# A graph and mixture-of-experts layer on one core: a helper matrix built on ScalarE, edge scatters started earlier, end-of-pass parts cut finer, a third buffer in the last stage, and seven slot one-hots in one comparison

## The reference, cut to what matters

```python
x0 = layernorm(x)
# graph: two hypergraph convolutions, four segment sums in all
m  = segment_sum((h @ W)[src], dst) / count(dst)     # then
h' = prelu(segment_sum(m[dst], src) / count(src) + b)
# linear attention over the nodes: k, v normalised per head, out = q (k^T v) / n
# mixture of experts on layernorm(x + graph + attention):
#   8 experts, the best 2 per token, y = sum_j w_j * (gelu(xn @ W1[e_j] + b1) @ W2[e_j] + b2)
```

## Time and profile before

| | |
|---|---|
| median of 3 runs | 5673.13 us (5672.77 to 5675.39) |
| profiled execution | 5671.47 us |
| its span | 5669.7 us |
| POOL busy | 3808.1 us (67%) |
| PE busy | 4272.6 us (75%) |
| DVE busy | 2923.7 us (52%) |
| ACT busy | 1244.4 us (22%) |
| mean granted PE clock | 0.878 |

### The profile page before, as it was taken

One profiled execution on the slowest core, in us unless ns is written; L12 is line 12 of the kernel. 1 busy time (PEld: TensorE's weight loads), 2 busy tenths in 40 slices (PEclk: granted clock), 3 DMA queues, 4 the chain that ended last, 5 costly groups with the idle time before them and its releaser, 6 DMA issues. The chain is left out here.

```text
span 5669.7 us, 68658 instructions
## 1 busy us (share of the span) xinstructions
PE 4272.6 (75%) x18010; PEld 2970.2 (52%) x18011; DVE 2923.7 (52%) x10203; ACT 1244.4 (22%) x3306; POOL 3808.1 (67%) x3968
## 2 busy tenths in 40 slices
PE   4799899999997878776566666655666665658994
PEld 2545566666665555554444444444444444445662
DVE  8788777777874555544333333333333333373334
ACT  0388655555531000000100000000000000132331
POOL 2777777777767777777677777777777777303442
PEclk9899999999998999897788888887778778778997
DMA  3400233333343333334454454344333333421115
GB/s 127 134 5 2 61 105 105 105 105 105 104 153 111 114 113 112 114 109 126 129 146 143 145 147 147 115 132 142 105 105 105 105 105 105 147 81 49 63 63 164
DMA packets 322940, 616.68 MB, mean 109 GB/s; under 512 B 79974, under 2 KB 199362, under 8 KB 322108
## 3 DMA queue, kind: packets, MB, share of 16 engines
q0 software_dynamic: 182400, 464.97, 28.7%
q1 hardware_dynamic: 66704, 75.75, 4.1%
q10 hardware_dynamic: 73516, 72.10, 3.9%
HBM read 525.54 MB, written 87.00 MB: 108 GB/s over the span
## 5 line engine op out<-in xcount | busy, mean ns | idle before, releaser
L594 POOL DMA_INDIRECT rowset<-table,idx x3324 | 3193.7, 961 | 1058.4 <-issue 1036.5
L1622 PE MATMUL PS<-rowset,ohg 128*128 x8192 | 2344.7, 441 | 1063.9 <-SPq L452 1046.2
L1622 PEld LDWEIGHTS PS<-rowset,ohg 128*128 128x128 f32 x8192 | 1752.9, 221 | 1596.0 <-issue 1301.6
L1156 DVE TENSOR_TENSOR rowset<-rowset,PS 128x257 f32 (+1 forms) x1024 | 430.7, 421 | 1926.0 <-PE PS L1622 1888.0
L1135 DVE TENSOR_SCALAR ohg<-iota,dl 128x128 f32<-128x128 f16 x4096 | 937.1, 308 | 30.8 <-issue 30.7
L1547 PE MATMUL PS<-region 128*128 128x416 f16 x3328 | 625.0, 339 | 0.0
L612 POOL DMA_INDIRECT scattered_d<-rowset x384 | 373.2, 972 | 221.5 <-DVE rowset L1031 100.6
L1547 PEld LDWEIGHTS PS<-region 128*128 128x128 f16 x3328 | 325.6, 98 | 257.6 <-issue 0.5
L693 ACT ACTIVATE region<-region 128x128 f16<-128x128 f16 x832 | 328.7, 395 | 478.0 <-DVE region L1059 477.1
L1058 DVE TENSOR_SCALAR region<-iota_c,region 128x832 f16<-128x832 f16 x832 | 400.6, 481 | 10.4 <-issue 10.2
L694 ACT ACTIVATE region<-region 128x128 f16<-128x128 f16 x832 | 320.9, 386 | 0.0
(11 more groups left out here) (321 smaller groups left out, 3175.1 us busy)
## 6 DMA issues: line engine op xcount, KB each, us to landing
rowset<-table,idx POOLq DMA_INDIRECT x3324, 2.8
table<-rowset ACTq DMA_DIRECT2D x21, 896.0 KB, 4.4
region<-xt_d ACTq DMA_DIRECT2D x98, 128.0 KB, 2.7
rowset<-ye_d SPq DMA_DIRECT2D x12, 1024.0 KB, 7.1
xpad_d<-rowset SPq DMA_DIRECT2D x1, 6272.0 KB, 21.4
xn_d<-rowset SPq DMA_DIRECT2D x49, 128.0 KB
xt_d<-rowset SPq DMA_DIRECT2D x49, 128.0 KB
table<-rowset SPq DMA_DIRECT2D x49, 128.0 KB
```

What stands on the lines that cost most here:

```text
L594: gp.indirect_dma_start(rowset[:, at + c % ring, 0:F], None, tables[p], bass.IndirectOffsetOnAxis(idx[p % 2][:, c:c + 1], 0)).then_inc(s_g ...
L1156: TT(a, a, pair_sum(p, v), ALU.add).then_inc(s_acc[p], 1)
L1622: m = MM(pair_sum(p, v), ohg[:, v * AG % RAW + j, :], rowset[:, ds(slot_of[v % U] + j, 1), 0:width(p)].rearrange("p a f -> p (a f)"), star ...
```

## The change

It has five parts. (a) POOL fills only a small 128 x 49 matrix `rows`, and ACT spreads it over 128 columns into `row_of` with one copy. (b) The packed edges are computed between the second and the third mask of `positions(0)`, and the places right after it, from their own 384-column chunk and slot numbers, before `fields(0)`. (c) The seven parts at the end of a pass become eight: blocks 42 to 48 are now 42 to 47 and 48 alone; ACT clears all seven parts of the next accumulator after its last store. In pass 1 the leaky part of blocks 42 to 47 is made after the last pair's sum, ahead of block 48. (d) The last stage has three `yl` buffers, which lie in `region`; the load of group q waits for group q - 3. (e) Seven slot one-hots are made by one two-tensor comparison, into the same ring.

```diff
+    PARTS = [(n * R7, (n + 1) * R7) for n in range(NR7 - 1)] + [(NB - R7, NB - 1), (NB - 1, NB)]
+    NP = len(PARTS)
+    YL = 3
-        yl = [gbuf_flat[:, n * 2 * G * F:(n + 1) * 2 * G * F]... for n in range(2)]
+        yl = [region[:, n * 2 * G * F:(n + 1) * 2 * G * F]... for n in range(YL)]
...
-                if q >= 2:
-                    sp.wait_ge(s_add, q - 1)
+                if q >= YL:
+                    sp.wait_ge(s_add, q - YL + 1)
...
+            select = ln["rows"][:, 0:NB]
+            link(gp.memset(select, 0.0))
+            link(gp.affine_select(out=select, in_=select, compare_op=ALU.not_equal, fill=float(P), base=0,
+                                  pattern=[[-1, NB]], channel_multiplier=1))
+            gp.affine_select(out=select, in_=select, compare_op=ALU.not_equal, fill=1.0, base=-HALF,
+                             pattern=[[-1, NB]], channel_multiplier=1).then_inc(s_const, 1)
...
-            link(gp.memset(row_of[:, :, :], 0.0))
-            link(gp.affine_select(out=row_of[:, :, :], in_=row_of[:, :, :], ..., pattern=[[-1, NB], [0, P]], ...))
-            gp.affine_select(out=row_of[:, :, :], in_=row_of[:, :, :], ...).then_inc(s_rows, 1)
...
-                pool.wait_ge(s_tab, p * 16 * NR7)
+                pool.wait_ge(s_tab, p * 16 * NP)
...
+            act.wait_ge(s_const, N_CONST - 1)
+            A(row_of, ln["rows"][:, 0:NB].unsqueeze(2).broadcast_to([P, NB, P]), ACT.Copy).then_inc(s_rows, 1)
...
             def end_pass(p, part=None):
-                for n in range(NR7):
-                    if n == NR7 - 1:
-                        act.wait_ge(s_acc[p], PAIR)
-                        clear(p + 1, 0).then_inc(s_zero, 1)
+                for n in range(NP):
                     if part is not None:
                         part(n)
                     store_part(p, n)
-                for n in range(1, NR7):
+                act.wait_ge(s_acc[p], PAIR)
+                for n in range(NR7):
                     clear(p + 1, n).then_inc(s_zero, 1)
...
+            def edge_codes():
+                c = first_part
+                link(TS(ti[:, 0, c], edges[:, 0, c], 1.0, None, ALU.add))
+                link(TS(ln["edge"], edges[:, 1, c], 13, None, ALU.logical_shift_left))
+                link(TT(ln["edge"], ln["edge"], ti[:, 0, c], ALU.bitwise_or))
+            def places():
+                c = first_part
+                link(V.tensor_copy(ti[:, 0, c], pos[:, c]))
+                link(TS(ti[:, 1, c], ti[:, 0, c], 7, None, ALU.logical_shift_right))
+                link(V.tensor_copy(chunk_of[0][:, c], ti[:, 1, c]))
+                link(TS(ti[:, 1, c], ti[:, 0, c], P - 1, None, ALU.bitwise_and))
+                link(V.tensor_copy(slot_of[0][:, c], ti[:, 1, c]))
+                link(STT(out=ln["place"], in0=slot_of[0][:, c], scalar=float(NC), in1=chunk_of[0][:, c], op0=ALU.mult, op1=ALU.add))
+                dve.sem_inc(s_places, 1)
...
+                    if o == 0 and b == AHEAD:
+                        edge_codes()
...
             positions(0)
+            places()
             fields(0)
-            c = slice(0, SC_FROM * U)
-            link(STT(out=ln["place"], ...))
-            link(TS(ti[:, 0, c], edges[:, 0, c], 1.0, None, ALU.add))
-            link(TS(ln["edge"], edges[:, 1, c], 13, None, ALU.logical_shift_left))
-            TT(ln["edge"], ln["edge"], ti[:, 0, c], ALU.bitwise_or).then_inc(s_places, 1)
...
-                if k == 1 or n == NR7 - 1:
+                if k == (n < NP - 1):
                     leaky(n)
...
-                TS(fc["ohs"][:, at, :], iota_h[:, :], fb_["slot"][:, c:c + 1], None, ALU.is_equal)
+                if c % ES == 0:
+                    TT(fc["ohs"][:, at:at + ES, :], iota_h[:, :].unsqueeze(1).broadcast_to([P, ES, P]),
+                       fb_["slot"][:, c:c + ES].unsqueeze(2).broadcast_to([P, ES, P]), ALU.is_equal)
```

More of the change, by code:

```diff
@@ L258, in gps_layer @@
             "mask": ((MR, EC), f16), "carry": ((EC,), f16), "behind": ((P,), f16), "spread": ((NB - 1 + P,), f16),
-            "blocks_before": ((P,), f16), "tot_b": ((2, P), f16), "minus": ((P,), f16)})
+            "blocks_before": ((P,), f16), "tot_b": ((2, P), f16), "minus": ((P,), f16), "rows": ((NB + 1,), f16)})
         at_places = 3 * R7 * F + 2 * NB + KT * F + KT * 2 * INNER + PAIRS * F
@@ L308, in gps_layer @@
         xT = carve(ohg_flat, {"xT": ((2, F), f32)})["xT"]
-        yl = [gbuf_flat[:, n * 2 * G * F:(n + 1) * 2 * G * F].rearrange("p (b j f) -> p b j f", b=G, j=2) for n in range(2)]
+        yl = [region[:, n * 2 * G * F:(n + 1) * 2 * G * F].rearrange("p (b j f) -> p b j f", b=G, j=2) for n in range(YL)]
         s_pad, s_const, s_rows, s_raw = sem("s_pad"), sem("s_const"), sem("s_rows"), sem("s_raw")
@@ L349, in gps_layer @@
         s_ys = [sem(f"s_ys{k}") for k in range(ER)]
-        s_yl = [sem(f"s_yl{k}") for k in range(2)]
+        s_yl = [sem(f"s_yl{k}") for k in range(YL)]
         sort_from = (SC_FROM, 0)
-        N_CONST = 14
+        N_CONST = 15
         MASKS_FROM, MASKS_TO, RANKS_TO, COLUMNS_FROM = 32, 56, 126, 140
@@ L728, in store_part @@
             def store_part(p, n):
-                act.wait_ge(s_fin, p * NR7 + n + 1)
-                act.dma_start(rows(tables[p + 1], n * R7, R7), accs[p % 2][:, n * R7:(n + 1) * R7, 0:F]).then_inc(s_tab, 16)
+                lo, hi = PARTS[n]
+                act.wait_ge(s_fin, p * NP + n + 1)
+                act.dma_start(rows(tables[p + 1], lo, hi - lo), accs[p % 2][:, lo:hi, 0:F]).then_inc(s_tab, 16)
             def end_pass(p, part=None):
-                for n in range(NR7):
-                    if n == NR7 - 1:
-                        act.wait_ge(s_acc[p], PAIR)
-                        clear(p + 1, 0).then_inc(s_zero, 1)
+                for n in range(NP):
                     if part is not None:
@@ L775, in negated @@
                 if n >= 2:
-                    act.wait_ge(s_fin, NR7 + n - 1)
-                A(negative[n % 2], accs[1][:, n * R7:(n + 1) * R7, 0:F], ACT.Relu, scale=-1.0).then_inc(s_hr, 1)
+                    act.wait_ge(s_fin, NP + n - 1)
+                lo, hi = PARTS[n]
+                A(negative[n % 2][:, 0:hi - lo, :], accs[1][:, lo:hi, 0:F], ACT.Relu, scale=-1.0).then_inc(s_hr, 1)
             end_pass(1, negated)
@@ L837, in _ @@
             act.dma_start(b1_d, b1_rows).then_inc(s_b1d, 16)
-            act.wait_ge(s_fin, 3 * NR7 + 1)
+            act.wait_ge(s_fin, 3 * NP + 1)
             act.dma_start(fa_["w2"], ffn_w2.rearrange("e (t p) f -> p e t f", p=P)).then_inc(s_fw2, 16)
@@ L1156, in acc_pass @@
                     TT(a, a, pair_sum(p, v), ALU.add).then_inc(s_acc[p], 1)
-                    if after is not None and v >= LAST_GROUP + R7 - 1:
-                        n, k = (v - LAST_GROUP - R7 + 1) // R7, (v - LAST_GROUP - R7 + 1) % R7
-                        after(n, k, v)
+                    if after is not None:
+                        for n, (lo, hi) in enumerate(PARTS):
+                            after(n, v - (LAST_GROUP + hi - 1), v)
             def part(p, n):
-                return accs[p % 2][:, n * R7:(n + 1) * R7, 0:F]
+                return accs[p % 2][:, PARTS[n][0]:PARTS[n][1], 0:F]
             def inverse(p, n):
-                s = slice(n * R7, (n + 1) * R7)
+                s = slice(*PARTS[n])
                 link(TS(inv[:, p, s], accs[p][:, s, F], 1.0, None, ALU.max))
@@ L1176, in mean @@
                         inverse(0, n)
-                    TT(part(p, n), part(p, n), inv[:, 0, n * R7:(n + 1) * R7].unsqueeze(2).broadcast_to([P, R7, F]),
+                    TT(part(p, n), part(p, n), inv[:, 0, lo:hi].unsqueeze(2).broadcast_to([P, hi - lo, F]),
                        ALU.mult).then_inc(s_fin, 1)
@@ L1232, in leaky @@
                 dve.wait_ge(s_hr, n + 1)
-                STT(out=part(1, n), in0=negative[n % 2], scalar=not_a, in1=part(1, n), op0=ALU.mult, op1=ALU.add).then_inc(s_fin, 1)
+                STT(out=part(1, n), in0=negative[n % 2][:, 0:PARTS[n][1] - PARTS[n][0], :], scalar=not_a, in1=part(1, n), op0=ALU.mult, op1=ALU.add).then_inc(s_fin, 1)
             def biased(n, k, v):
@@ L1238, in biased @@
                     inverse(1, n)
-                    for b in range(n * R7, (n + 1) * R7):
+                    for b in range(*PARTS[n]):
                         m = STT(out=accs[1][:, b, 0:F], in0=accs[1][:, b, 0:F], scalar=inv[:, 1, b:b + 1], in1=vecs[:, 0, :],
@@ L1455, in _ @@
                         x2 = accs[1][0:m, q * G + b, 0:F]
-                        a = STT(out=x2, in0=yl[q % 2][0:m, b, j, :], scalar=wt[0:m, j, q * G + b:q * G + b + 1], in1=x2,
+                        a = STT(out=x2, in0=yl[q % YL][0:m, b, j, :], scalar=wt[0:m, j, q * G + b:q * G + b + 1], in1=x2,
                                 op0=ALU.mult, op1=ALU.add)
```

16 lines of the change are left out of this document (6 added, 10 removed).

## The result

The changed kernel takes 5630.07 us (median of 4, 5625.86 to 5636.64), the kernel before 5674.26 (5672.77 to 5678.6) beside it: a ratio of 0.9922, 95% interval 0.9905 to 0.9939, so 35 to 54 us less. The profiled execution took 5630.74 us, its span 5629.0; against the profiled one of before the span is 40.7 us shorter.

| stretch | before | after | gain | predicted |
|---|---|---|---|---|
| start to first gather | 629.00 | 612.85 | 16.15 | 18.2 |
| pass 0 with its seam | 1072.72 | 1072.17 | 0.55 | 3.3 |
| pass 1 with its seam | 1071.77 | 1067.23 | 4.54 | 4.2 |
| pass 2 with its seam | 1063.90 | 1061.21 | 2.69 | 3.3 |
| pass 3 to the sort of tokens | 1230.66 | 1228.61 | 2.05 | 0 |

A forecast was written before the change was run, and what follows sets the result against it. Four passes of POOL gathers, three quarters of the span, were taken as the bound, untouched inside a pass. Gains of 18.2 + 11 + 1.8 + 15 = 46 us from 5671.5 gave 5625.5, by median 5626; range 5614 to 5642.

The forecast's parts named there:

- (a): Start of the kernel: DVE stops waiting behind POOL's wide writes, first mask at 12.3 instead of 27.3, gain 15.0 us.
- (b): Ahead of the first gather: scatters start 5.0 us earlier, of which 3.2 us are left at the first gather.
- (c): Seams after passes 0, 1 and 2: the finer last part gains 3.3, 4.2 and 3.3, in sum 11 us.
- (d): Last stage: with three buffers DMA becomes the bound, 12 us over ten groups and some 3 at the end, 15 us.
- (e): Sort of tokens: one comparison for seven columns gains 0.13 us in each of 14 groups, 1.8 us.
- likeliest case: Whole kernel: the terms come as summed, 5626 us, own range 5618 to 5636, chance 0.70.
- the hold: POOL's scatters at column 32 wait for the second order's first mask, about 2 us, leaving 3.2 of 5.0 us.
- the landing: Seams of passes 0 and 2: the smaller 128 KB store lands in 2.7 us against 4.4, gain 1.7 us each.
- The rival: Sort of tokens: the one comparison costs what its elements cost, a loss of 10 us, 5638; chance 0.06.
- the last wait: End of the last stage: the last load is requested one group sooner, some 3 of DVE's 4.3 us wait go.
- loads of the last stage stretch to 10 us: Last stage: a sign named in advance that would show the prediction wrong.
- The slower rival: Pass 0: if PE's clock is throttled to 0.93, PE sets the pace, some 80 us more, 5706; chance 0.03.

The follow-up runs named there:

- undo_a: The changed kernel with POOL's three wide operations over `row_of` back, ACT's copy and the narrow constant gone: 6679.66 us, ratio 0.9965 to the kernel before.
- control: The changed kernel, unedited, run at a mean TensorE clock of 0.79: 6670.76 us, ratio 0.9946 to the kernel before.

## Why the prediction was right

Right in time (5630 for 5626), in sign and in its likeliest case. By its own steps:

- **(a)** Forecast 15.0, all of stage 1 shifted. PE starts 15.06 us earlier, as computed, and undo_a gives it back. At the first predicated copy 13.9 are left: PE's 98 histogram matmuls took 19.94 us instead of 18.95. The difference lies at their start: they come 0.35 us apart for 4.8 us instead of 2.7, and 0.18 apart after that. In the kernels with this same start the 98 took 18.96 to 20.51, so that 1 us varies from run to run and does not belong to the change. ACT's copy took 5.43 us (5.9 forecast) and nobody waited for it.
- **(b)** Forecast 5.0 to the scatters; 5.5 measured (70.0 less 64.5 from the first copy). Its own terms left 3.0 of them at the hold (168.3 less 165.3), where it wrote 3.2. Of these, at the first gather, 2.1 came (16.15 less 14.07, the shift at the end of the scan at 32.52). The hold at column 32 was 2.60 us with the usual 0.30 of issue in it, 2.0 forecast; what eats the rest between 152 and 606 us (later holds, up to 2.05 us) was not taken apart. DVE still waits 3.33 us for the table, so the scatters still bound.
- **(c)** The step that failed: "Gain 1.6 + 1.7 = 3.3 per seam, in passes 0 and 2". It holds in pass 2 (2.7) and not in pass 0 (0.55), because the 1.7 for the landing came from medians over the whole execution, the 2.7 even from loads, and at the end of pass 0 the store had been following SP's 2 MB by timing alone. DVE's 1.6 did come there: the last store is issued about 1.3 us behind the last sum instead of 3.0. But the 128 KB then took 5.9 us to land where the 896 KB had taken 4.5, a loss of 1.4 in place of the gain of 1.7. The trace of the kernel before shows SP's loads at that seam. Pass 1 gave 4.5 for 4.2, and that is in part luck: from the last sum to the next gather it gave 5.9 (13.04 to 7.16), but the last sum came 7.86 us behind the pass's last gather instead of 5.78, of which the forecast had 0.3. PE's last eight matmuls took 3.62 us at a granted clock of 0.55 there, against 2.00 at 1.00 before. In sum 7.8 instead of 11, still in the bounds of 6 and 13.
- **(e)** The pace of neighbours (0.165 us a piece), not the durations shown, gave 2.53 us a step: measured 2.53, and 1.9 us for 1.8. The rival took the elements as the price. The new form takes 1.09 us, as its nearest row did, and the old one was paid per instruction: 0.165 us for 128 elements, where the rows of 896 and 1792 elements give a fixed 0.16. By the Trainium skill's tier table alone ("VectorE: DVE Perf Modes", "The perf-mode tier table") 10 us would have been lost (the prediction's estimate); the trace has 1.9 gained.
- **(d)** 15 forecast, 15.8 measured, and by the mechanism named: 1.57 MB per group at 390 to 400 GB/s, 4.0 us forecast, 3.93 measured. Its two terms were off and made up for each other: the groups gave 13.9 instead of 12 (the first of them run at DVE's own 3.3 us, and there are eleven steps, not ten), the last wait 1.9 instead of 3 (4.35 to 2.49 us). But the sign set against it, "loads of the last stage stretch to 10 us", was badly chosen. They stretched to 8.3 to 10.3, as they must: with three in flight and one group per 3.93 us a load lasts 3 x 3.93 - 3.38 = 8.4; with four, 12.3.
- **Not in the sum:** +2.05 ahead of the sort of tokens and -3.00 in the experts. Windows of before and after (the third column from the right is the granted clock):

```profile
4922.00:4926.00 4.00, 4.00 (x22) 4.00 (x20) 3.71 (x6) 2.13 (x3) 0.00 (x0) 0.50 0.41 141
...
5137.00:5141.00 4.00, 2.42 (x11) 1.48 (x11) 0.85 (x2) 1.77 (x4) 0.95 (x1) 1.00 0.00 0
```

```profile
4896.00:4900.00 4.00, 1.68 (x8) 1.68 (x9) 2.22 (x6) 3.13 (x5) 0.00 (x0) 0.81 0.87 295
4904.00:4908.00 4.00, 3.19 (x15) 2.47 (x13) 3.04 (x25) 0.65 (x2) 0.00 (x0) 1.00 0.46 143
...
5109.00:5113.00 4.00, 2.42 (x9) 1.69 (x9) 0.85 (x2) 1.77 (x4) 0.94 (x1) 0.50 0.00 0
5113.00:5117.00 4.00, 4.00 (x8) 2.18 (x7) 0.75 (x2) 0.34 (x1) 0.01 (x1) 0.51 0.12 33
```

  At the same work (26 us earlier after the change) the clock stands at 0.50 before and 0.81 to 1.00 after, and in the experts the other way round: the first pair of chunks ran at full clock before, at half after. Over the whole of each stretch: from the last sum of pass 3 to the sort of tokens the granted clock is 0.76 before and 0.79 after, and the stretch takes 177.8 instead of 181.1 us (pass 3 itself took 1.3 more). The experts start at 0.50 in both, for 15.0 us before and 23.1 after. A shift of 24 to 28 us moved the work against the change of clock level. That both terms are of the clock is read from these rows, no run tested it; that they cancel to 1 us is chance.
- **The slower rival** (PE's clock in pass 0) did not come: the window 790 to 840 stood at 1.00 after as well. The chips of the experiments show its direction, not its price: in the control, pass 0 stands at 0.91 in the stretch read above and takes 1359 us with its seam instead of 1072. By the rival's own sum 0.91 would cost 105 us (1060/0.91 - 1060), not 287, so a lower granted clock came with more than the clock alone explains.

## What to carry to other kernels

When a transfer is moved earlier, look at what was draining just ahead of it: its landing time is that of its new neighbourhood, not of the median row. In a stage bound by transfers add buffers until the rate stands still and then stop; a longer load is then no sign of harm. Cut a transfer whose rows don't divide well (106 into 96 and 10): here that took 5 us off the end of a stage, where putting the slow piece in the middle cost 1.

## What the runs showed that was not expected

The same kernel ran at mean granted clocks of 0.88 and 0.79, 5674 and 6705 to 6765 us, with the bound of pass 0 moving from POOL to PE; the change kept its sign and about its size. The slower runs came later, on four chips, and it is not known on which chip the first ones ran, so whether the chip or the time makes the difference is not shown. And a load of 106 rows uses about an eighth of the DMA rate when it runs alone (49 to 51 of 399 GB/s); placed among full ones it delays the next group by 2.4 us more than the usual 0.55. That fits a stage whose bytes count per engine and not in sum.
